# Where the last PV product of a pass stands among the transposes of the next pass

## What is computed

```python
x = x + attention(layernorm(x))       # 32 heads of 128, causal
x = x + ffn(layernorm(x))             # a linear layer and a routed low-rank term

# attention, cut to what matters
q = x @ w_q; k = x @ w_k; v = x @ w_v     # k, v: 8 heads, each used by 4 query heads
lq = x @ w_lq
lk = lq @ w_lk; lv = x @ w_lv             # 32 latent heads
q, k, lk = rope(q), rope(k), rope(lk)
attn = softmax(causal(q @ k.T * SCALE)) @ v
lat  = softmax(causal(q @ lk.T * SCALE)) @ lv
return attn @ w_o + lat @ w_lo
```

## Time and profile before

| what | value |
|---|---|
| median of 3 runs | 2184.03 us |
| the 3 runs | 2177.3 to 2184.62 us |
| span of the profiled execution, first to last instruction | 2180.9 us |
| PE busy | 2099.1 us, 96% |
| DVE busy | 1582.3 us, 73% |
| ACT busy | 1141.3 us, 52% |
| POOL busy | 884.5 us, 41% |
| PE instructions | 11236 matmuls |

### The profile page before, as it was taken

How to read it: one execution, slowest core, us unless ns; L and a number is a source line. 1 busy time by engine, 2 the same in 40 slices (tenths; PEclk the granted TensorE clock), 3 DMA queues, 4 the chain that set the end, 5 groups by cost and what they waited for, 6 DMA issues and landing times.

```text
span 2180.9 us, 37717 instructions
## 1 busy us (share of the span) xinstructions
PE 2099.1 (96%) x11236; PEld 1757.8 (81%) x11236; DVE 1582.3 (73%) x2946; ACT 1141.3 (52%) x2502; POOL 884.5 (41%) x693
## 2 busy tenths in 40 slices
PE   5999999999999999999999999999999999999989
PEld 4888878888788887888888887888878888888877
DVE  6677767777777777777767776777777777777775
ACT  2555545555455555556455554555545555455541
POOL 4333443434533344443533444333453434444311
PEclk9999999999999999999999999999999999999999
DMA  2111111111111111111111111111111111111121
GB/s 94 36 35 36 38 30 41 41 36 45 27 41 27 41 46 31 41 31 41 36 35 34 39 36 32 41 39 38 44 28 41 27 41 46 30 41 31 41 50 39
DMA packets 101898, 84.34 MB, mean 39 GB/s; under 512 B 28200, under 2 KB 73896, under 8 KB 101680
## 3 DMA queue, kind: packets, MB, share of 16 engines
q1 hardware_dynamic: 101680, 81.65, 15.3%
HBM read 79.26 MB, written 2.36 MB: 37 GB/s over the span
## 4 chain that ended last, share of the span: by engine, by line
PE 69%; DVE 14%; issue 10%; POOL 3%; ACT 3%; DVEq 0%; DMA 0%; ACTq 0%; SPq 0%; POOLq 0%
PE scores L415 9%; PE scores L417 8%; PE scores L416 8%; PE bankT L477 8%; PE bankX L415 7%; PE bankX L417 6%; PE bankX L416 6%; PE bankO L415 5%; PE bankO L417 5%; PE bankO L416 5%; DVE rot_half L980 3%; DVE rot_half L979 3%; DVE probs L963 3%; DVE PT_lo L969 2%; DVE o_raw L1034 1%
## 5 line engine op out<-in xcount | busy, mean ns | idle before, releaser
L703 ACT ACTIVATE PT_hi<-bankT 128x512 fp32r<-128x512 f32 (+2 forms) x640 | 337.0, 533 | 424.2 <-PE bankO L417 356.4
L969 DVE TENSOR_TENSOR PT_lo<-bankT,PT_hi 128x512 fp32r<-128x512 f32 (+2 forms) x640 | 387.7, 609 | 196.6 <-ACT PT_hi L703 191.6
L762 ACT ACTIVATE probs<-probs,nmax 128x128 f32<-128x128 f32 (+7 forms) x512 | 394.8, 773 | 140.5 <-DVE nmax L963 140.1
L963 DVE CUSTOM_DVE_ANT_0 probs<-scores,mask 128x128 f32<-128x128 f32 (+7 forms) x512 | 381.0, 750 | 64.6 <-PE scores L417 61.8
L477 PE MATMUL bankT<-ident,probs 128*128 128x128 f32 x2304 | 381.9, 275 | 10.3 <-ACT probs L762 4.4
L477 PEld LDWEIGHTS bankT<-ident,probs 128*128 128x128 f32 x2304 | 280.9, 140 | 93.6 <-ACT probs L762 18.6
L1197 POOL TENSOR_TENSOR rot<-rot,cos 128x512 f32<-128x512 f32 x144 | 185.7, 1289 | 230.5 <-DVE rot_half L980 230.5
L1191 POOL TENSOR_TENSOR OT_lo<-o_raw,OT_hi 128x512 fp32r<-128x512 f32 x64 | 82.7, 1292 | 411.6 <-ACT OT_hi L703 411.6
L1199 POOL TENSOR_TENSOR rot<-rot,rot_half 128x512 f32<-128x512 f32 x144 | 207.3, 1440 | 11.3
L703 ACT ACTIVATE OT_hi<-o_raw 128x512 fp32r<-128x512 f32 x128 | 80.9, 632 | 187.1 <-DVE o_raw L1034 182.8
L979 DVE TENSOR_TENSOR rot_half<-rot,sin 64x512 f32<-64x512 f32 x144 | 108.8, 755 | 82.8 <-ACT rot L703 79.3
(11 more groups left out here) (241 smaller groups left out, 5213.3 us busy)
## 6 DMA issues: line engine op xcount, KB each, us to landing
inv_b<-inverses SPq DMA_DIRECT2D x128, 256.0 KB, 4.0
stage<-in_L_attn_w_q SPq DMA_DIRECT2D x32, 256.0 KB, 4.4
stage<-in_L_attn_w_lv SPq DMA_DIRECT2D x32, 256.0 KB, 2.7
stage<-in_L_attn_w_o SPq DMA_DIRECT2D x32, 256.0 KB, 4.3
stage<-in_L_attn_w_lo SPq DMA_DIRECT2D x32, 256.0 KB, 2.6
acc<-in_L_attn_hidden_states SPq DMA_DIRECT2D x2, 1024.0 KB, 6.6
stage<-in_L_attn_w_k SPq DMA_DIRECT2D x8, 256.0 KB, 4.5
stage<-in_L_attn_w_v SPq DMA_DIRECT2D x8, 256.0 KB, 4.6
```

The costliest lines, as they stand in the source:

```text
L703: return act.activation(place, src, ACT.Copy)
L762: act.activation(prob_tile(c, t), prob_tile(c, t), ACT.Exp, bias=nmax[:, c, t:t + 1], scale=-1.0, accum_out=rsum[:, c, t:t + 1]).then_inc( ...
L963: dve.tensor_tensor_reduce(place, src, tile_view(mask[:, S - width:S], c), -SCALE, -MASKED, ALU.add, ALU.min, nmax[:, c, t:t + 1]).then_in ...
L969: dve.tensor_tensor(pt_place(1, hh, w, j), bankT[j % 2][:, block_columns(c, j):CH], f32(pt_place(0, hh, w, j)), ALU.subtract).then_inc(pt_ ...
```

## The change

On PE, PV-last is issued ahead of T0, for all passes. The order at a turn goes from T0, PV-last, T1 to PV-last, T0, T1. Nothing else is edited: no other engine's order, no buffer, no semaphore, no transfer.

```diff
                             elif hh == 0:
                                 pe.wait_ge(x_free, g * FREES_PER_GROUP + FREES_BEFORE)
-                        if s == BLOCKS[w] - 1:
-                            next_transposes(0)
                         pv_block(g, hh, w, s)
+                    next_transposes(0)
                     next_transposes(1)
```

## The result

| kernel | median, us | runs, us |
|---|---|---|
| before | 2182.87 | 2176.9 to 2184.98 (13) |
| changed | 2188.29 | 2184.48 to 2190.14 (13) |

The account below looks back on a forecast made before the run. PE was taken to bound the kernel, busy 2099.1 of 2180.9 us, the change acting only through waits at turns. Losses of 9.0 and 0.36 us, other terms 0, summed to 9.4 us: forecast 2193.4 us, range 2184 to 2201.

Parts of the forecast that it names:

- Part 1: Turns from pass 1 to 2: T0 starts 0.36 us later, behind PV-last's three MATMULs; T1's end stays.
- Part 2: Turns from pass 1 to 2: the chain behind T0 delays the third score tile 0.36 us, 25 times, 9.0 us.
- Part 3: Turns from pass 3 to 0: T0's wait is filled but reappears before PV0; 0 to 0.7 us in all.
- The end of the seventh group: Where the loop falls through to the last group without the idle wait: one full loss of 0.36 us.
- Part 4: Turns from pass 0 to 1: 7.0 us of wait move from T0 to the projection; net 0.
- Part 5: Turns from pass 2 to 3: T0 moves by 0.36 us, covered by 1 us of waiting for DVE's rotation; 0.
- The covered waits are kept: Turns from passes 0 and 3: T0's waits, 15.0 us, become gain; 2169.0 us, or 2178.4 with the loss; chance 0.07.
- Nothing moves: Turns from pass 1 to 2: the 0.36 us are absorbed, say by ACT or DVE; 2184 us; chance 0.14.
- T0 is late at turns from pass 3 too: Turns from pass 3: T0's full 0.36 us delays `scale_out` and PV0; 8.6 us more, 2202.0 us; chance 0.14.
- The clock: Eight transposes in a row bring a half-clock stretch in each head; 54 us, 2248 us; chance 0.03.

Follow-up runs that it names:

- a2: PV-last ahead of T0 only at turns from pass 1 to 2, the order of before at the others; 2189.81 us, 1.0046 of the kernel before.
- a3: PV-last ahead of T0 at all turns except those from pass 1 to 2; 2181.23 us, 0.9999 of the kernel before.
- a4: T0 and T1, then PV-last, at every turn, against the kernel before; 2180.77 us, 1.0001 of it.
- c1: Changed kernel with T0 and T1 at turns from pass 1 to 2 held behind the new pass's first score tile; 2211.47 us, 1.0139 of before.
- a1: The changed kernel, unedited, run again beside the kernel before; 2191.05 us, 1.0049 of the kernel before.
- b2: Changed kernel with DVE's `scale_out` ahead of block 0's low part at turns from passes 1 and 3; 2156.9 us, 0.9886 of before.

## Why the prediction was nearly right

**Part 1, right.** T0 came 0.36 us later (0.23 to 0.59), and T1 ended where it did.

**Part 2, right in its mechanism, too large.** It foresaw 25 x 0.36 = 9.0 us; the intervals hold 7.5 us, 0.30 us per turn. The links moved by 0.36, 0.35, 0.35 and 0.33 us (T0, high part, low part, end of `scale_out`), and the third score tile by 0.34 us. About 0.02 us were lost because `scale_out` took 1.07 instead of 1.09 us, and more behind the wait: the next score product starts 97.02 - 96.31 = 0.71 us into the tile after, and 0.73 us before. The shift is only 0.32 us from there on. In the prediction's own signs, the distance to the third score tile was 0.70 us of the 0.73 foretold, and that tile stood at 4.86 us of the 4.88. The chain was right but it isn't perfectly stiff, and the term lacked these few hundredths, which 25 turns make 1.5 us. That the loss sits here and nowhere else is shown by a2 and a3, that it comes from T0 and not from PV-last by a4, and that it goes on at the same rate by c1.

**Part 3, right.** PV0 stayed at 3.58 us against 3.57, the gap at T0 closed and opened again at PV0, and the sum over 24 turns was +0.3 us of the 0 to 0.7 expected. The end of the seventh group took 0.34 us of the 0.36.

**Part 4, right.** The projection stayed at 2.26 us against 2.25, and its idle wait was 0.65 us where about 0.6 was foretold.

**Part 5, right.** The sum behind turns from pass 2 to 3 was -0.6 us over 24, nothing.

**The total.** 7.5 + 0.3 + 0.3 us, with the -0.1 of the two other turns, make 8.0 us for the change, where the prediction had 9.4. The spans differ by only 4.0 us. Most of what lies between is clock. The first turn comes at 71.85 instead of 74.28 us, 2.4 us sooner: ahead of it the profile before has the granted clock at 0.50 from 34.91 to 41.74 and from 62.22 to 65.63 us, the changed one only from 35.77 to 39.18. The half-clock stretch of the earlier trace rows didn't occur, which takes 1.8 us out of one interval. The other turns of the loop are 0.5 us shorter together and the remaining intervals 0.1, and behind the last turn come 0.8 us more, where the changed profile is at half clock for 3.4 us longer. Then 8.0 - 2.4 - 1.8 - 0.5 - 0.1 + 0.8 = 4.0.

Of the 5.1 us between 2193.4 and 2188.29, 1.2 aren't of the change at all: the prediction started from the median of three runs, 2184.03, and the median of thirteen is 2182.87. Its 3.1 us between span and time held this too; the profiled execution of the changed kernel has 1.8 us there (2186.74 and 2184.9). The rest, 4.0 us, is 9.4 against a difference of medians of 5.4.

The medians differ by 5.4 us in the first measurement and by 9.3 in the second, of one and the same kernel. Both intervals hold a loss of 7.4 us (0.34%), if only at their edge; 8.0 us (0.37%) lies just above the first one. The time of an execution goes with its mean granted clock. Of the kernel before, beside a1, eight executions at a clock of 0.995 have a mean of 2182.5 us, and four at 0.998 have 2176.7. Compared at one clock, the changed kernel in a1 costs 8.5 us at 0.995 (2191.0, four executions, against 2182.5) and 8.4 at 0.997 (2186.8, one, against 2178.4, four), near the 8.0 us of the traces. How much of the gap between the two measurements is a different mix of clocks stays open, since the clocks of the kernel before aren't on record for the first.

Two smaller things. The prediction had every engine's busy sum the same; PE's was 9.4 us shorter, which fits short waits that counted as busy time before and now show as idle time; ACT's was 7.0 us shorter (1141.3 to 1134.3), and the cause of that is open. And its chance of over 0.5% slower, 0.33, isn't the sum of what it names: a third of 0.62, with 0.14 and 0.03, is 0.38.

**The rivals.** *The covered waits are kept* falls with a3: 15.0 us of wait went from T0 to the projection and PV0 (7.9 and 7.1 us more there), and the ratio was 0.9999. The Trainium skill, Perfetto Trace Analysis, section Optimization Strategy, would have the gap on the busiest engine closed; here the gap closed and no time came of it, until the instruction that ended the next gap was moved too, in b2. *Nothing moves* falls with a2 and c1. *T0 is late at turns from pass 3 too* falls with the 3.58 us and the +0.3 us. *The clock* falls with a4 and with the profile after: the granted clock over the heads is 1.00 with seven or eight transposes in a row at each turn, and in all ten profiles each stretch of half clock among the passes comes right after the loop's entrance or one of its turns. By the Trainium skill, TensorE: Matmul & The Clock Gate, Part 4: PE-mode transpose, these don't count as products do; no run here lost clock at these turns by them.

## What to carry to other kernels

When a moved instruction fills a wait of the busiest engine, look at the next wait behind it before counting a gain: if that one ends with another engine, the time only changes its place in the list of waits. When the instruction that finishes sooner has a reader that stands in order behind something else, the order of both engines is one decision. Here PE's alone lost up to 9 us, DVE's alone gave 4, and both gave 25 (1.1%).

## What the hardware did that I had not expected

The one stretch of half clock in the earlier trace rows isn't a property of the kernel. Such stretches of 3.4 us come at turns of the loop, different ones in each execution. Counted from the first turn between passes to the last, the profile before has one, the two of the changed kernel have none, a3 has two. One more can come at the entrance of the loop, in front of the first turn: in the profile before, which the earlier trace rows doesn't show, and in a1 from 63.84 us, but not in the other profile of the changed kernel. Here is that of before, and then the two of a3 (the same columns as in the earlier trace rows):

```profile
62.22:65.63 3.41, 3.39 (x12) 3.00 (x12) 2.81 (x7) 0.98 (x3) 1.51 (x2) 0.50 0.02 1
...
1360.97:1364.38 3.41, 3.41 (x11) 2.90 (x10) 1.43 (x4) 1.63 (x4) 0.78 (x1) 0.50 0.07 5
...
1620.40:1623.80 3.40, 3.40 (x13) 2.92 (x12) 1.31 (x4) 1.09 (x2) 1.28 (x1) 0.50 0.10 13
```

The granted clock there is 0.50, the 1.2 GHz level, after PE had stood idle at the turn of the loop (the earlier trace rows has 1.93 us of that) or at its entrance, where it stood idle for 1.00 us. The same 1.00 us in the changed kernel, up to 61.31, was followed by a clock of 1.00, so the idle time alone doesn't decide. The interval between turns that holds the stretch of before is 1.8 us shorter in the changed kernel, close to the half of 3.4 us. A change worth a few microseconds should be read from distances inside the heads, not from two spans.
